# Two more pair sums by accumulating transfers in attention, two sums less on TensorE, and wide products for scale and offset

## The reference, cut to what matters

```python
scale  = t_emb @ w_scale                       # (2, 1, 512)
offset = t_emb @ w_offset
h = layer_norm(x) * scale + offset
q = h @ wq / sqrt(512); k = h @ wk; v = h @ wv # 16 heads of 32
q, k = rotary_pos_emb(q), rotary_pos_emb(k)
a = softmax(einsum('bhik,bhjk->bhij', q, k))   # 2 x 16 x 2048 x 2048
y = einsum('bhij,bhjv->bhiv', a, v)
x = x + y @ wo                                 # then a gelu MLP, then a second layer
```

## Time and profile before

| what | us |
|---|---|
| median of 3 runs | 3592.47 |
| lowest and highest of the 3 | 3590.37, 3604.18 |
| the profiled execution's own time | 3593.72 |
| span of the profile | 3591.9 |
| mean granted TensorE clock over the span | 0.98 |
| TensorE busy | 3431.2 (96%) |
| VectorE busy | 2077.5 (58%) |
| ScalarE busy | 1514.0 (42%) |
| GpSimd busy | 2018.6 (56%) |

### The profile page before, as it was taken

One profiled execution on the slowest core, in us unless ns is written; L12 is line 12 of the kernel. 1 busy time (PEld: TensorE's weight loads), 2 busy tenths in 40 slices (PEclk: granted clock), 3 DMA queues, 4 the chain that ended last, 5 costly groups with the idle time before them and its releaser, 6 DMA issues. The chain is left out here.

```text
span 3591.9 us, 47122 instructions
## 1 busy us (share of the span) xinstructions
PE 3431.2 (96%) x16672; PEld 2241.0 (62%) x16672; DVE 2077.5 (58%) x3325; ACT 1514.0 (42%) x2789; POOL 2018.6 (56%) x1613
## 2 busy tenths in 40 slices
PE   7999899999999999999999959999999995999998
PEld 5777445545454545545455438888888883778876
DVE  5776677777777777777777435222222213354554
ACT  2332366666666666666666732111111112122121
POOL 3654388798878978888888812222222223343342
PEclk9999999999999999999999979999999997999999
DMA  4555686868778686877865543222222213222221
GB/s 173 182 172 203 119 152 118 156 134 143 145 139 156 121 156 133 142 144 140 155 123 106 120 139 88 79 68 74 71 71 62 69 36 132 86 87 77 72 87 42
DMA packets 176737, 419.32 MB, mean 117 GB/s; under 512 B 15382, under 2 KB 62998, under 8 KB 151670
## 3 DMA queue, kind: packets, MB, share of 16 engines
q1 hardware_dynamic: 153606, 249.59, 26.4%
q0 software_dynamic: 22896, 166.73, 24.0%
HBM read 162.25 MB, written 87.03 MB: 69 GB/s over the span
## 5 line engine op out<-in xcount | busy, mean ns | idle before, releaser
L845 DVE TENSOR_REDUCE part_max<-ps_att 128x1 f32<-128x512 f32 x1972 | 1226.8, 684 | 381.6 <-PE ps_att L763 381.5
L891 ACT ACTIVATE probs<-ps_att 128x512 f32<-128x512 f32 x2048 | 1063.6, 603 | 533.1 <-PE ps_att L735 469.8
L942 POOL TENSOR_TENSOR prob_sums<-prob_sums,probs 128x512 f32<-128x512 f32 x884 | 1142.9, 1536 | 55.2 <-DMA probs<-probs 55.2
L787 PE MATMUL ps_att<-probs,v_tok 128*32 128x512 f32 x4096 | 547.2, 606 | 0.0
L1433 POOL TENSOR_TENSOR ff_g_lo<-ff_g,ff_g_hi 128x512 fp32r<-128x512 f32 x128 | 165.6, 1294 | 548.2 <-DVE ff_g_hi L1394 548.2
L735 PE MATMUL ps_att<-q_stack,k_first 97*128 97x512 f32 x768 | 326.6, 425 | 6.1 <-ACT probs L891 5.8
L735 PE MATMUL ps_att<-q_stack,k_stack 97*128 97x512 f32 x768 | 321.0, 426 | 8.1 <-ACT probs L891 7.5
L1302 ACT ACTIVATE ff_g<-ps_ff 128x512 f32<-128x512 f32 x128 | 76.8, 600 | 578.5 <-PE ps_ff L1186 578.5
L763 PE MATMUL ps_att<-k_first,q_stack 96*128 96x512 f32 x756 | 302.5, 400 | 7.3 <-DMA q_stack<-qk 7.3
L763 PE MATMUL ps_att<-k_stack,q_stack 96*128 96x512 f32 x768 | 303.6, 395 | 0.0
L1923 POOL TENSOR_TENSOR av_gated_lo<-av_full,av_gated_hi 128x512 fp32r<-128x512 f32 x64 | 94.5, 1477 | 313.8 <-ACT av_gated_hi L1760 313.8
(11 more groups left out here) (205 smaller groups left out, 5528.0 us busy)
## 6 DMA issues: line engine op xcount, KB each, us to landing
probs<-probs POOLq DMA_DIRECT2D x159, 1024.0 KB, 8.6
q_stack<-qk SPq DMA_DIRECT2D x144, 128.0 KB, 7.0
qk<-rot_hi SPq DMA_DIRECT2D x64, 256.0 KB, 6.5
qk<-rot_lo SPq DMA_DIRECT2D x64, 256.0 KB, 2.5
av_gate_rows<-gate SPq DMA_DIRECT2D x64, 256.0 KB
k_stack<-qk SPq DMA_DIRECT2D x24, 512.0 KB, 10.7
k_first<-qk SPq DMA_DIRECT2D x18, 512.0 KB, 10.7
x_in_sb<-in_x SPq DMA_DIRECT2D x8, 1024.0 KB, 7.0
```

Of the source, the lines that this page charges most:

```text
L787: mm = nc.tensor.matmul(o_ps[rows, :], t["v"][:, steps[w]["b"], k, rows], t["p"][:, w % PR, h, :], start=(k == 0), stop=(k == LT - 1))
L845: nc.vector.tensor_reduce(t["pm"][:, r, k:k + 1], mx[mx_uses % 3], AX.X, ALU.max)\
L891: nc.scalar.activation(t["p"][:, at % PR, h, :], sT[(at * G + h) % 3], ACT.Exp)\
L942: nc.gpsimd.tensor_tensor(x, first, t["p"][:, w % PR, h, :], ALU.add).then_inc(s["acc_done"], 1)
```

## The change

In attention, TensorE sums no tile of its own any more, but in the last block; seven pairs go by transfer in place of five, and GpSimd takes tiles 4 and 13 singly. The rounds stay eight and move to other steps; the last pair of a block is issued, and its last three rounds are done, in the next block. The K and V loads move, the sums of a block are finished at step 10 in place of 5 of the next one, a third semaphore serves the pairs, and one more job of maxima moves into `prepare`. For scale and offset the condition becomes the stationary side and the weights are streamed 512 wide, into two column groups; the two resulting rows are copied to SBUF and turned by eight small transposes. For the first block, rounding to fp32r moves from ScalarE to VectorE.

```diff
-PE_SUMS = (8, 14)
-PAIRS = (0, 3, 6, 9, 12)
-POOL_FIRST = 2
-POOL_ROUNDS = ((5, 0), (7, 5), (9, 3), (11, 6), (12, 11), (14, 9), (16, 15), (18, 12))
+PE_SUMS = ()
+PAIRS = (0, 2, 5, 7, 9, 11, 14)
+POOL_FIRST = 4
+POOL_ROUNDS = ((5, 0), (7, 2), (10, 5), (12, 7), (14, 9), (16, 11), (18, 13), (20, 14))
-LAST_SUMS = (8, 11, 12, 13, 14, 15)
+LAST_SUMS = (11, 12, 13, 14, 15)
-K_AT = (2, 6, 10, 14, 18, 22)
-V_AT = (26, 30)
-LAST_AT = 5
+K_AT = (2, 6, 9, 18, 22, 25)
+V_AT = (34, 38)
+LAST_AT = 10
-AHEAD = JOBS + 3
+AHEAD = JOBS + 4
...
+                def modulation():
+                    for k in range(DC):
+                        for v, w in enumerate((wa, wb)):
+                            mm = nc.tensor.matmul(ps[32 * v:32 * v + B, 6, :], cond[:, k, :], w[:, k, :],
+                                                  start=(k == 0), stop=(k == DC - 1))
+                    mm.then_inc(s["vec_rows"], 1)
+                    pe.wait_ge(s["vec_kept"], 2)
+                    for v in range(2):
+                        for f in range(DC):
+                            at = (v * DC + f) * B
+                            mm = nc.tensor.transpose(ps[:, 7, at:at + B], vrow[0:B, v, f * P:(f + 1) * P], c["ident"][0:B, 0:B])
+                    mm.then_inc(s["vec_done"], 1)
...
-                for v, w in enumerate((wa, wb)):
-                    for f in range(DC):
-                        at = (v * DC + f) * B
-                        mm = vectors(ps[:, 7, at:at + B], w, f)
-                mm.then_inc(s["vec_done"], 1)
+                modulation()
...
+                dve.wait_ge(s["vec_rows"], 1)
+                for v in range(2):
+                    nc.vector.tensor_copy(vrow[0:B, v, :], ps[32 * v:32 * v + B, 6, :]).then_inc(s["vec_kept"], 1)
...
+                for f in range(DC):
+                    dve.wait_ge(s["full"], f + 1)
+                    nc.vector.tensor_copy(hh[:, 0, f, :], hf[:, f, :]).then_inc(s["hi"], 1)
...
-                affine(0, 0)
-                affine(0, 1)
-                weight_hi(0)
-                weight_hi(1)
-                affine(0, 2)
-                affine(0, 3)
-                for u in range(2, len(pieces)):
+                for f in range(DC):
+                    affine(0, f)
+                for u in range(len(pieces)):
                     weight_hi(u)
...
-        return s[f"paired{m % 2}"], 16 * (m // 2 + 1)
+        return s[f"paired{m % 3}"], 16 * (m // 3 + 1)
...
             def last_sums(n):
+                opening = not shares(n)[0]
+                if opening and n:
+                    pe.wait_ge(s["l_kept"], n)
...
-                if at < end and k - 2 in PAIRS and not by_pe(at - 2):
-                    add_pair(n, k - 2)
+                if 2 <= at < end and (at - 2) % LT in PAIRS and not by_pe(at - 2):
+                    add_pair((at - 2) // LT, (at - 2) % LT)
```

More of the change, by code:

```diff
@@ L108, in prepare @@
         ff, q1 = hf, hl[:, 0, 0, :]
+        vrow = rot
         kept = vst[:, 0].rearrange("p g j n -> p (g j n)").rearrange("p (i n) -> p i n", i=4)
@@ L111, in prepare @@
                   for i in range(3) for f in (0, 2)]
-        s = phase(nc, ctx, "pre_cond_in pre_w_in pre_ident_set pre_mem_set pre_vec_done pre_vec_out pre_tab_in0 pre_tab_in1 "
+        s = phase(nc, ctx, "pre_cond_in pre_w_in pre_ident_set pre_mem_set pre_vec_rows pre_vec_kept pre_vec_done pre_vec_out pre_tab_in0 pre_tab_in1 "
                            "pre_wq_in0 pre_wq_in1 pre_w_hi pre_w_lo pre_x_in0 pre_x_in1 pre_stats pre_aggr pre_var pre_root "
@@ L230, in wait_bank @@
                     i = at_use[kind, number]
+                    if i == 4:
+                        pe.wait_ge(s["vec_kept"], 2)
                     if i == 5:
@@ L474, in affine @@
                                          scale=sc_v[:, f, n // NB:n // NB + 1]).then_inc(s["full"], 1)
+                    if n == 0:
+                        return
                     act.wait_ge(s["full"], u + 1)
@@ L793, in sums @@
                 n, k = w // LT, w % LT
-                if k == PE_SUMS[0] and n:
+                opening = shares(n)[0].index(k) == 0
+                if opening and n:
                     pe.wait_ge(s["l_kept"], n)
@@ L798, in sums @@
                     mm = nc.tensor.matmul(l_ps[h * KD:(h + 1) * KD, :], c["ones"][:, 0:KD], t["p"][:, w % PR, h, :],
-                                          start=(k == PE_SUMS[0]), stop=False)
+                                          start=opening, stop=False)
                 mm.then_inc(s["psum"], 1)
             def last_sums(n):
+                opening = not shares(n)[0]
+                if opening and n:
+                    pe.wait_ge(s["l_kept"], n)
                 pe.wait_ge(s["acc_done"], POOL_ADDS * n + G * len(shares(n)[1]))
@@ L806, in last_sums @@
                     mm = nc.tensor.matmul(l_ps[h * KD:(h + 1) * KD, :], c["ones"][:, 0:KD], t["acc"][:, n % 2, h, :],
-                                          start=False, stop=True)
+                                          start=opening, stop=True)
                 mm.then_inc(s["sum_done"], 1)
@@ L937, in add_round @@
                             pool.wait_ge(s["sum_done"], n - 1)
+                        pool.wait_ge(s["exp"], (n * LT + POOL_FIRST) * G + h + 1)
                         first = t["p"][:, (n * LT + POOL_FIRST) % PR, h, :]
@@ L970, in attention @@
         names = ("q_in0 q_in1 q_in2 q_in3 q_first1 q_first2 v_first k_in v_in mx_full mx_free neg_max max_set0 max_set1 "
-                 "score exp pv psum acc_done paired0 paired1 l_in recip rl_stored sum_done o_kept l_kept y_stored l_stored "
+                 "score exp pv psum acc_done paired0 paired1 paired2 l_in recip rl_stored sum_done o_kept l_kept y_stored l_stored "
                  "ones_set")
```

## The result

The changed kernel takes 3620.24 us, median of 7 runs (3608.12 to 3623.73), against 3591.38 us for the kernel before in the same comparison (7 runs). The ratio is 1.0059, 95% interval 1.0045 to 1.0073: slower by about 0.6%. The quotient of the two medians is 1.0080 and lies above that interval: five of the seven runs before lie at 3590 to 3592 us and two at 3600 and 3604, so their median sits at the low end. The loss lies at 0.6 to 0.8%. Its profiled execution took 3620.24 us with a span of 3618.4 us, 26.5 us more than the span before.

The account below looks back on a forecast made before the run. TensorE was taken to set the pace before, the DMA engines to become as scarce or scarcer; 3593.7 us with +5, -6 and -3 gave 3589.7, or 3588 against the median; range 3545 to 3635 us.

Parts of the forecast that it names:

- Part 1: Attention, TensorE: losing two of three sums saves 1.74 us a block, pace 199.3 us a unit; last unit gains 6 us.
- Part 2: Attention, GpSimd: 45.5 us of rounds and issues fit a block of 49.8, with some 5 us of slack.
- Part 3: Attention, DMA transfers: engines as scarce as TensorE or scarcer; 210 us a unit, +5 us over seven units.
- the carrying over: Attention, blocks with K pieces: some 5 us of delay can be carried over, so 210 us a unit, not 215.3.
- rival 3: Attention: engines bound where K comes in, nothing carried, 215.3 us a unit; 3627 us, 3641 with half-clock stretches; chance 0.30.
- Who yields: Attention, DMA queues: pair transfers yield to SP's loads, which held 86.9% of the engines against 16.5%.
- rival 2: Attention: SP's loads yield and the excess spreads over the unit, 204 us a unit; 3548 us; chance 0.19.
- Part 4: Start, before attention: wide products, first rounding on VectorE, four extra maxima; together -3 us, between -8 and +4.

Follow-up runs that it names:

- early issue: The changed kernel with GpSimd issuing each pair between the second and third addition of the round ahead, not behind that round: 3546.95 us, ratio 0.9862.
- spread loads: The changed kernel with early issue and K pieces at steps 3, 10, 20, 26, 34, 39, V at 50, 56 of a unit: 3512.47 us.

## Why the prediction was wrong, point by point

I forecast 3588 us, no change. The kernel takes 3620.24, outside the forecast's own 3567 to 3611 and inside the range of 3545 to 3635. The loss is attention's: a unit takes 215.2 us where I took 210.

**Part 1 was right.** Single tiles are summed only in the last block, undisturbed blocks take 49.9 to 50.4 us, the last unit gained 6.1 us for the 6 forecast.

**Part 2 was right in its numbers and wrong in what I made of them.** The work fits (waits excluded), and the slack exists where nothing disturbs: with K pieces nearly empty the round for tiles 14 and 15 ends 18.2 us into the next block in most blocks (18.6 forecast), 4.7 us before ScalarE's last head of that slot. In the changed kernel the same round ends at 21.2 to 30.7 us, and in 21 of 24 blocks nothing of the slack is left; even in the fourth blocks, which fetch no K, it ends at 22.8 to 24.7. But I had written myself that each round waits for its pair and the next issue stands behind that round, and did not follow it: for four of a block's seven pairs one round and one more issue (about 6.2 us) stand between issue and use, while no pair lands in less than 6.9 us and the median is 9.1. Where K pieces come in, two rounds are not enough either: ahead of the rounds for tiles 0 and 2 GpSimd waits 2.4 to 4.6 us in the mean of the first and of the second blocks. Once late, it does not catch up; its waits for TensorE ahead of an issue are gone.

**Part 3: the price was right, the carrying over was the step that failed.** A pair held the engines for 5.45 us in the fifth unit; the first two blocks were to want 57.8 us each without carry, and took 56.6 and 56.5; a unit without carry was put at 215.3 us and measured 215.2. The failing step is the sentence "What can be carried is the slack of part 2, some 5 us: I take 210 us a unit". Nothing was carried: the slack that was to carry it was spent in the fourth block already, ahead of the next unit's K pieces (part 2). That was rival 3, forecast at 3627 us with chance 0.30; measured 3620. Its place (the blocks with K pieces) and its price were right. Its stated reason, that the engines are the bound, is only half: early issue ran the same transfers in 205.7 us, and with spread loads in 200.3. The engines' time sets how crowded a block is; whether the excess can move on to the next block depends on how early the pairs are in the queue.

That 215.3 and 215.2 agree so well is partly luck. The first two blocks came out 2.5 us below their 115.6, the other two 2.4 us above their 99.7. The sum also had nothing for the clock, which rival 3 priced apart. At a mean of 0.96 in the first two blocks, some 9 us of a unit ran at the lower level; as an estimate, that costs 4.5 us a unit at the most, and no run separates it from the waits. The first unit, which I had counted with the others, did not lose: it took 226.5 us from SP's first load of attention, for 227.1.

**Who yields.** I took from the earlier trace rows that pairs yield to SP's loads, and held it against rival 2. I had misread the rows. In those 12 us two pairs played a part, one issued at 1031.73 and one at 1044.34 (timeline of GpSimd; then the queues from 1037 to 1039 and from 1039 to 1049, kernel before):

```profile
1031.73 1.16 POOL L924 DMA_DIRECT2D probs<-probs  x1
1044.34 0.90 POOL L924 DMA_DIRECT2D probs<-probs  x1 [1.49 <-ACT probs L891]
...
q0 software_dynamic: 32, 0.26, 98.1%
...
q1 hardware_dynamic: 566, 1.33, 104.2%
q0 software_dynamic: 16, 0.00, 0.2%
```

The 16.5% are the end of the first pair, which had the engines to itself until 1039 although SP had issued loads since 1034.85. Then SP's loads had them, and the second pair moved nothing up to 1049. So in this stretch what was issued first went first, and the row does not show a pair that yields. Where both queues had packets, in the changed kernel from 892 to 894, it looks different:

```profile
q0 software_dynamic: 46, 0.38, 90.3%
q1 hardware_dynamic: 46, 0.09, 13.6%
```

Here they take turns, packet for packet, and the pair with its larger packets has nine tenths of the time. The Trainium skill's page "DMA: Bandwidth & Descriptors", section "Queues, rings and completion order", has the engines go round between queues packet by packet. These two microseconds agree with that, where I had set the rule aside, if a packet of the profile is what the page calls one; the five from 1044 to 1049, in which SP's queue alone was served with a pair issued, do not show it. With early issue it is SP's loads that slip (2.17 MB in a first block for 2.89). That this comes from pairs being in the queue earlier fits all these rows; why a newly issued pair sometimes waits some 5 us for its first packet stays open.

**Part 4 was too timid.** The wide products took 4.5 us, near the lower bound of 4, not 7; the first projection came 9.5 us earlier for the 5 forecast. The four extra maxima cost 7.26 - 4.88 = 2.4 us as forecast. Attention began 5.6 us earlier. That lead was gone at the end of the first block (its copy at 459.01 for 458.93); the second block, 55.3 us for 60.2, brought most of it back. The 3.2 us more behind attention appear in none of the terms; where that stretch was compared in other runs it lay 1.0 us below to 1.5 us above the kernel before, so I leave it as unexplained spread.

**What stays open.** Why a stall falls on some second blocks and not on others with early issue (49.9 to 58.2 us) is not settled; the clock's fall behind a long wait adds to the long ones (0.94 in the three longest), and I did not separate the two.

## What to carry to other kernels

When an engine both issues transfers and consumes them in one ordered stream, its busy time says little: count how long a transfer is under way against the work that stands between its issue and its use, and move the issue ahead of work, not behind it. See then who waits for the work that the issue now interrupts: with five pairs it was TensorE, and the time rose. Removing work that stands between them can buy nothing, since it was the cover. A shared resource at 97% can be no bound at all if the traffic without a due time is allowed to slip, and a placement that does little while another wait binds should be tried again once that wait is gone.

## What the runs showed of the hardware that I had not expected

- An adding transfer within SBUF costs 1.8 times a copy of the same size: 5.44 us (70.9% of 1300 us for 177.61 MB, changed kernel) against 2.98 us of all 16 engines for 1 MB, landing after 9.1 against 5.3 us.
- The recorded share of the DMA engines passes 1 in crowded blocks (1.03 over first blocks with early issue), and a pair's packets are then recorded as longer (5.62 us against 5.19 in quiet blocks). A share of 1.0 in such a window is no proof that no more would fit; my 57.8 us leaned on it.
- With packets of both queues at hand the engines took turns between them, 46 and 46 packets in 2 us, and the queue with the larger packets had 90.3% of the time.
- Two fp32 products with two stationary columns each, in different column groups, ran at once: eight products of 512 columns, recorded as sixteen, in 4.5 us, the first records of a group 0.8 us and the later ones 0.43 us apart.
